# Statistics of the next input moved ahead, softplus in three steps, and a shorter tie rule, in a one-core kernel of AdaLN, Mamba and mixture of experts

## The chip, the cores and the metric

The kernel runs on one core of a Trainium2 chip. The time is the device time of one execution in microseconds (us). The kernel before has a median of 687.32 us over 3 runs (684.01 to 691.07). The execution that was profiled took 684.8 us, its span from the first to the last instruction being 683.1 us.

## What is computed

Eight sequences of 512 tokens with 128 features pass through two blocks. All values are fp32.

```python
mod = (silu(c) @ wmod)            # six rows per sequence: sa, ca, ga, sb, cb, gb
h = layernorm(x) * (1 + ca) + sa
# Mamba: d_inner 256, state 16, dt_rank 8
xz = h @ in_proj_w.T;  x, z = split(xz)
x = silu(conv1d(x) + conv_b)      # causal, 4 taps, per channel
dt, Bm, Cm = split(x @ x_proj_w.T)
delta = softplus(dt @ dt_w.T + dt_b)
h_t = h_(t-1) * exp(delta * A) + (delta * x) * Bm     # 256 x 16 states, 512 steps
y = sum_n(h_t * Cm) + x * D;  y = y * silu(z)
x = x0 + ga * (y @ out_proj_w.T)
# mixture: a shared expert and 8 experts, the two likeliest weighted by their softmax
h = layernorm(x) * (1 + cb) + sb
x = x + gb * (shared(h) + sum_e(weight_e * expert_e(h)))   # gelu(h @ w1 + b1) @ w2 + b2
```

When two experts have the same probability, the one with the lower index comes first.

## The kernel before

One sequence is called a batch (b). Its tokens are 4 tiles of 128 (NT); the 256 inner channels are 2 halves (Q). The recurrence of a batch is cut into 16 units (UN, `u` from 0 to 15): a unit is one half of the channels and two of the sixteen states, 128 partitions by 2 x 512 elements.

What a unit needs, engine by engine: ScalarE (ACT) computes the decay exp(delta * A) by two instructions of 128x511 (`decays`, L885); VectorE (DVE) multiplies into PSUM (`scan_input`, L1197) and runs the recurrence (`scan`, L1206); GpSimd (POOL) multiplies by C (`readout`, L433); TensorE (PE) adds the product, transposed, to y in PSUM by eight transposes (`y_add`, L516). There are 8 decay buffers and 4 state buffers, so that `scan(b, u)` waits for `y_add(b, u - 4)`. PSUM has one input buffer for the scan.

Every engine runs its own list of instructions in the order in which the functions `slots` issue them; there is no scheduler. `pipeline` calls `slots(b, a, n, m)` with four batches at different stages: b is scanned (all 16 units), a = b - 1 goes through the gate, the output projection and the mixture of experts, n = b + 1 through convolution, projections and softplus, m = b + 2 through its input statistics and normalisation. One such call is called a period here; after the first, b = 0 (no a), there are seven, five of them with all four, one without m (b = 6) and one without n and m (b = 7), and a tail for the last a.

The stages of a in a period, in order: `gate_y` (DVE), `g_transpose` (PE), `g_rows` (ACT), `out_proj` (PE), `att_rows` (ACT, L969), `att_transpose` (PE, L600), `residual` (DVE, L1226: the add, then mean and variance of x1), `make_rstd` (POOL, L420 and L423: the power -0.5), `x1hat` (DVE, L1244), `x1_transpose` (PE, L616), `h2_rows` (ACT, L992 and L995), `router` (PE, L624), `split_h2` and `logits` (DVE, L1310 and from L1254), 18 times `up` (PE, L645 to L647, three matmuls each) with `gelu` (ACT, L1014), `top2` (DVE, from L1268), then 8 times `down` (PE, L677), `mix_scaled` (ACT, L980) and `mix_add` (PE, L687). `gelu` and Exp need different tables of ScalarE. `keep_busy` (L611) is a row of transposes whose result nobody reads.

The stages of n: `conv_in`, `x_silu` (ACT, L906), `x_proj`, `dt_proj` (PE, L572, one for each half), `softplus_relu` and `softplus_abs` (ACT, L936 and L943), `softplus_exp` (ACT, L952), `softplus_log` (ACT, L957) and on DVE `make_delta` (L1170 to L1179). The softplus is relu(v) + e - ((1 + e) - 1) + ln(1 + e), with e = exp(-|v|). The stages of m: `load_x` (SP queue, L347), `stats` (DVE, from L1147), `make_rstd`, `xhat` (DVE, L1158).

In `readout` the flag `paced` makes POOL wait for the input of the next unit as well as for its own scan, so that the readout lies beside a scan and not beside a `scan_input`.

## Time and profile before

| | before |
|---|---|
| median of 3 runs | 687.32 us (684.01 to 691.07) |
| profiled execution | 684.8 us, span 683.1 us |
| busy: PE, DVE, ACT, POOL | 593.3, 598.3, 489.7, 320.2 us |
| chain that ended last, share of the span | PE 53%, DVE 31%, issue 7%, ACT 5%, POOL 2% |
| mean granted clock of TensorE | 0.955 of full speed |
| starts of `residual` (L1226), a = 0 to 7 | from 118.0 us to 636.6 us |

A busy time is the time in which an engine runs instructions. Two engines are busy for nearly nine tenths of the span, so neither alone tells what a shorter instruction is worth: for that one follows one period through all engines. In a timeline, a bracket behind an instruction gives the idle time of its engine ahead of it and the instruction whose end ended it. Consecutive instructions overlap by about a tenth of a microsecond, so that lengths can add up to a little more than the difference of the starts. The times of a timeline are counted from the start of the span.

### The profile page before, as it was taken

What the parts mean: (1) busy time and instruction counts of PE and PEld (TensorE: products, weight loads), DVE (VectorE), ACT (ScalarE), POOL (GpSimd) and SP (SyncE); (2) the same over time, 40 slices, a digit from 0 to 9 for tenths busy, and PEclk for the clock granted to TensorE, in tenths of its full rate; (3) what the DMA queues carried; (4) which work ended last, traced back from release to release, by engine and by line L of the source; (5) the groups of instructions that cost most, each with busy time, mean ns of one, the idle gap of its engine ahead of it and who ended that gap; (6) DMA issues with size and microseconds to landing.
All of it is one profiled execution on the core that took longest, in us unless ns stands there. A gap on an engine that the chain in (4) does not pass through costs nothing.

```text
span 683.1 us, 9767 instructions
## 1 busy us (share of the span) xinstructions
PE 593.3 (87%) x3646; PEld 466.5 (68%) x3646; DVE 598.3 (88%) x713; ACT 489.7 (72%) x861; POOL 320.2 (47%) x171
## 2 busy tenths in 40 slices
PE   5684478899989998999989998999979947998897
PEld 4243345689657965788567966787668936798686
DVE  5399999999999999999999999999998999798416
ACT  3689535999589976989589957998598925962460
POOL 1036556446654556446653656446543664464000
PEclk9787589999999999999999999999999968999999
DMA  7423333314432235133531343223522442220000
GB/s 221 161 92 140 123 139 142 125 70 169 163 128 82 108 128 184 62 124 124 173 124 63 124 160 138 83 103 124 179 103 70 176 156 83 103 78 16 1 1 16
DMA packets 26705, 77.87 MB, mean 114 GB/s; under 512 B 3025, under 2 KB 17570, under 8 KB 18466
## 3 DMA queue, kind: packets, MB, share of 16 engines
q1 hardware_dynamic: 26178, 76.82, 31.1%
q8 instruction: 29, 0.48, 0.3%
q10 hardware_dynamic: 480, 0.43, 0.2%
q14 instruction: 18, 0.15, 0.1%
HBM read 74.61 MB, written 2.62 MB: 113 GB/s over the span
## 4 chain that ended last, share of the span: by engine, by line
PE 53%; DVE 31%; issue 7%; ACT 5%; POOL 2%; DMA 1%; DVEq 0%; POOLq 0%; ACTq 0%
DVE state L1206 15%; PE psum L677 12%; PE psum L516 10%; DVE psum L1197 8%; PE psum L543 5%; PE psum L645 5%; PE psum L647 4%; PE psum L646 4%; PE psum L687 3%; POOL state L433 2%; PE psum L662 2%; PE psum L565 1%; ACT L866 1%; DVE out_sb L1244 1%; PE psum L799 1%
## 5 line engine op out<-in xcount | busy, mean ns | idle before, releaser
L433 POOL TENSOR_TENSOR state<-state,bc 128x1024 f32<-128x1024 f32 x127 | 300.1, 2363 | 291.8 <-DVE psum L1197 291.8
L1206 DVE TENSOR_TENSOR_SCAN state<-decay,psum 128x1024 f32<-128x1024 f32 x128 | 292.2, 2283 | 21.9 <-PE psum L516 9.5
L885 ACT ACTIVATE decay<-delta,a_neg 128x511 f32<-128x511 f32 x256 | 166.1, 729 | 10.4 <-DVE state L1206 10.3
L516 PE MATMUL psum<-ident,state 128*128 128x128 f32 x1024 | 139.0, 283 | 33.6 <-POOL state L433 33.4
L1197 DVE TENSOR_TENSOR psum<-bc,du 128x1024 f32<-128x1024 f32 x128 | 157.6, 1231 | 4.8 <-DVE state L1206 0.5
L516 PEld LDWEIGHTS psum<-ident,state 128*128 128x128 f32 x1024 | 120.3, 146 | 56.0 <-POOL state L433 44.9
L677 PE MATMUL psum<-down_w,h 128*128 128x128 f32 x896 | 109.9, 276 | 0.0
L677 PEld LDWEIGHTS psum<-down_w,h 128*128 128x128 f32 x896 | 104.4, 192 | 5.3 <-issue 5.3
L1014 ACT ACTIVATE h<-psum,vec 128x512 f32<-128x512 f32 x144 | 97.0, 688 | 2.1 <-PE psum L647 0.6
L980 ACT ACTIVATE gT_mix<-psum,w 128x128 f32<-128x128 f32 x224 | 64.8, 388 | 20.0 <-PE psum L687 14.4
L645 PE MATMUL psum<-h_hi,up_hi 128*128 128x512 f32 x144 | 59.2, 411 | 10.7 <-DVE h_lo L1310 6.7
L543 PE MATMUL psum<-h_sb,conv_in_wT 128*128 128x512 f32 x128 | 59.9, 614 | 8.8 <-ACT h_sb L895 8.8
L647 PE MATMUL psum<-h_hi,up_lo 128*128 128x512 f32 x144 | 57.7, 401 | 0.0
L646 PE MATMUL psum<-h_lo,up_hi 128*128 128x512 f32 x144 | 57.6, 400 | 0.0
L543 PEld LDWEIGHTS psum<-h_sb,conv_in_wT 128*128 128x128 f32 x128 | 24.3, 199 | 34.6 <-issue 25.4
L645 PEld LDWEIGHTS psum<-h_hi,up_hi 128*128 128x128 f32 x144 | 27.5, 191 | 20.5 <-DVE h_lo L1310 7.3
L687 PE MATMUL psum<-ident,gT_mix 128*128 128x128 f32 x224 | 33.9, 274 | 0.0
L647 PEld LDWEIGHTS psum<-h_hi,up_lo 128*128 128x128 f32 x144 | 27.4, 190 | 6.7
L646 PEld LDWEIGHTS psum<-h_lo,up_hi 128*128 128x128 f32 x144 | 27.6, 191 | 6.0
L687 PEld LDWEIGHTS psum<-ident,gT_mix 128*128 128x128 f32 x224 | 26.0, 141 | 1.5 <-ACT gT_mix L980 1.5
L611 PE MATMUL psum<-ident 128*128 128x128 f32 x210 | 26.2, 273 | 0.0
L906 ACT ACTIVATE du<-psum,vec 128x512 f32<-128x512 f32 x16 | 10.8, 687 | 21.2 <-PE psum L543 18.7
(151 smaller groups left out, 638.3 us busy)
## 6 DMA issues: line engine op xcount, KB each, us to landing
bc<-bc_rows SPq DMA_DIRECT2D x64, 1024.0 KB, 4.7
x_sb<-_attn_hidden_states_dram SPq DMA_DIRECT2D x9, 256.0 KB, 2.8
x<-_attn_hidden_states_dram SPq DMA_DIRECT2D x7, 256.0 KB, 3.0
out_dram<-out_sb SPq DMA_DIRECT2D x7, 256.0 KB, 2.4
h<-in_L_ffn_rw_dram SPq DMA_DIRECT2D x1, 1024.0 KB
bc_rows<-rows SPq DMA_DIRECT2D x8, 64.0 KB, 4.8
h<-in_L_wmod_dram ACTq DMA_DIRECT2D x1, 384.0 KB
h<-in_L_attn_in_proj_w_dram SPq DMA_DIRECT2D x1, 256.0 KB, 4.7
```

Of the source, the lines that this page charges most:

```text
L433: pool.tensor_tensor(state[:, u % STATE_RING, :, :], state[:, u % STATE_RING, :, :], bc[:, pair % BC_RING, 1, first:first + NU, :], ALU.mu ...
L516: last = nc.tensor.matmul(Y[q][:, t * P:(t + 1) * P], state[:, u % STATE_RING, s, t * P:(t + 1) * P], ident[:, :], start=False, stop=(u in ...
L543: last = nc.tensor.matmul(A[q], conv_in_wT[:, q, k, :], h_sb[:, k:k + L], start=(k == 0), stop=(k == KC - 1))
L645: nc.tensor.matmul(bank, high, h2_hi[:, :], start=True, stop=False)
L646: nc.tensor.matmul(bank, high, h2_lo[:, :], start=False, stop=False)
L647: nc.tensor.matmul(bank, low, h2_hi[:, :], start=False, stop=True).then_inc(up_done, 1)
L677: last = nc.tensor.matmul(A[j % 2][:, e * DM:(e + 1) * DM], h1[:, (group * EG + e) * HQ + q, ts], down_w[:, group * EG + e, q, :], start=( ...
L687: last = nc.tensor.matmul(OUTP[:, t * P:(t + 1) * P], mix[:, j % 2, e, :], ident[:, :], start=False, stop=(j == DOWNS - 1 and e == EG - 1) ...
L885: last = nc.scalar.activation(decay[:, r, s, 1:L], delta[:, b.p, q, 1:L], ACT.Exp, scale=a_neg[:, q, k:k + 1])
L1014: nc.scalar.activation(h1[:, m, :], UP_RING[m % 3], ACT.Gelu, bias=vec[:, bias:bias + 1]).then_inc(gelu_done, 1)
L1197: nc.vector.tensor_tensor(IN, bc[:, pair % BC_RING, 0, first:first + NU, :], du[:, b.p, q:q + 1, :].broadcast_to([P, NU, L]), ALU.mult).th ...
L1206: nc.vector.tensor_tensor_scan(state[:, u % STATE_RING, :, :].rearrange("p n t -> p (n t)"), decay[:, u % DECAY_RING, :, :].rearrange("p n ...
```

## The change

- `top2`: in place of a comparison for equality, one for greater, a product with the mask `before` and a sum, the probabilities are multiplied by `tie_scale` (1 - 2^-24 where the other index is lower, else 1) and compared once: two instructions of 128x256 in place of four.
- Softplus: ScalarE computes 1 + e (`softplus_one`) into the last two buffers of h1; DVE takes relu + e and then ((1 + e) - 1) less that sum after unit 4, and subtracts it from the logarithm after unit 7. The instruction L1173 goes. The first batch keeps the form of before. `gelu` of the last two h1 buffers waits until DVE has read them.
- DVE: `residual`, `stats` of m and `x1hat` come in one piece between units 2 and 3; `split_h2` and `logits` after unit 3 in place of unit 4. `stats` has a buffer of its own (`bn_in`).
- PE: `att_transpose` ahead of both `dt_proj`; `y_add` of unit 2 ahead of the first `keep_busy`; the two `keep_busy` have 8 and 10 transposes in place of 14 and 5 (12 in the last period).
- POOL: the readout of unit 2 isn't paced when there is an a, and both `make_rstd` follow it.
- ACT: the decays are computed 7 units ahead in place of 6, and two units rather than four of them stand between softplus and the gelus; the other two follow in the loop over the experts and at its end.

```diff
...
 GATE_MIN = 0.25
 STATE_RING = 4
 DECAY_RING = 8
-AHEAD = 6
+AHEAD = 7
...
-        before = sb("before", [P, E, E], mybir.dt.bfloat16)
+        tie_scale = sb("tie_scale", [P, E, E])
...
         bn = sb("bn", [P, NT, 6])
+        bn_in = sb("bn_in", [P, NT, 6])
...
+
+        one_plus_e = h1[:, M_UP - Q:M_UP, :]
...
+        sp_one = sem("softplus_one_plus_exp")
...
+        def delta_steps(n, k):
+
+            return k if n.i == 0 else 3 + 2 * (n.i - 1) + k
...
-            pool.memset(before[:, :, :], 1.0).then_inc(const_made, 1)
+            pool.memset(tie_scale[:, :, :], 1.0 - 2.0 ** -24).then_inc(const_made, 1)
...
+            pool.affine_select(out=tie_scale[:, :, :], in_=tie_scale[:, :, :],
+                               pattern=[[1, E], [-1, E]],
+                               compare_op=ALU.is_gt, fill=1.0, base=0,
...
                 for u in range(UN - 1):
                     if b:
-                        readout(b, u)
+                        readout(b, u, paced=not (a and u == 2))
                     if a and u == 2:
                         make_rstd(1, stats2_done, rstd2_eps, rstd2_done, a)
-                    if m and u == 5:
+                    if m and u == (2 if a else 5):
                         make_rstd(0, stats_done, rstd_eps, rstd_done, m)
...
+                if a:
+                    att_transpose(a)
                 if n:
                     dt_proj(n, 0)
-                if a:
-                    att_transpose(a)
-                if n:
                     dt_proj(n, 1)
                 if b and a:
                     y_add(b, 0)
                 if b:
                     y_add(b, 1)
-                if a:
-                    keep_busy(a, n, 14)
+                    y_add(b, 2)
+                if a:
+                    keep_busy(a, n, 8)
                     x1_transpose(a)
-                if b:
-                    y_add(b, 2)
-                if a:
-                    keep_busy(a, n, 5 if b else 12)
+                    keep_busy(a, n, 10)
                     router(a)
                     for k in range(M_UP):
...
+            def softplus_one(n):
+                if n.i >= 3:
+                    act.wait_ge(shared_done, n.i - 2)
+                act.wait_ge(sp_exp, n.i + 1)
+                nc.scalar.activation(one_plus_e, g_soft[:, :, :], ACT.Identity,
+                                     bias=1.0).then_inc(sp_one, 1)
+
...
-            def gelu(a, m):
+            def gelu(a, m, n=None):
                 act.wait_ge(up_done, M_UP * a.i + m + 1)
+                if n and m == M_UP - Q:
+                    act.wait_ge(delta_step, delta_steps(n, 2))
...
+                if n and n.i > 0:
+                    softplus_one(n)
+                if a:
+                    h2_rows(a)
+                if b:
                     decays(b, AHEAD + 1)
-                if a:
-                    h2_rows(a)
-                if b:
-                    decays(b, AHEAD + 2)
-                    decays(b, AHEAD + 3)
                 if a:
                     router_e(a)
                     load_gelu_table(a)
                     for k in range(M_UP):
-                        gelu(a, k)
+                        gelu(a, k, n)
                     weights_out(a)
...
                 for j in range(DOWNS - 1):
-                    if b and j < DOWNS - 2:
-                        decays(b, AHEAD + 4 + j)
+                    if b:
+                        decays(b, AHEAD + 2 + j)
...
-                    last = nc.vector.bn_stats(bn[:, t, :], x_sb[:, t, :])
+                    last = nc.vector.bn_stats(bn_in[:, t, :], x_sb[:, t, :])
...
                 for t in range(NT):
-                    last = nc.vector.bn_aggr(mean_var[:, 0, t, :], bn[:, t, :])
...
+            def relu_plus_exp(n):
                 d = delta[:, n.p, :, :]
                 dve.wait_ge(sp_relu, Q * n.i + Q)
                 dve.wait_ge(sp_exp, n.i + 1)
-                nc.vector.tensor_tensor(d, d, e, ALU.add).then_inc(delta_step, 1)
-                dve.wait_ge(delta_step, 3 * n.i + 1)
+                nc.vector.tensor_tensor(d, d, g_soft[:, :, :], ALU.add).then_inc(delta_step, 1)
+
+            def rounded_less_sum(n):
+                d = delta[:, n.p, :, :]
+                dve.wait_ge(delta_step, delta_steps(n, 1))
+                dve.wait_ge(sp_one, n.i)
+                nc.vector.scalar_tensor_tensor(out=d, in0=one_plus_e, scalar=1.0, in1=d,
+                                               op0=ALU.subtract, op1=ALU.subtract
+                                               ).then_inc(delta_step, 1)
+
+            def log_less(n):
+                dve.wait_ge(delta_step, delta_steps(n, 2))
                 dve.wait_ge(sp_ln, n.i + 1)
+                for q in range(Q):
+                    nc.vector.tensor_tensor(delta[:, n.p, q, :], skip[:, q, :],
+                                            delta[:, n.p, q, :], ALU.subtract
+                                            ).then_inc(delta_done, 1)
+
...
-                k = 8 * a.i
+                k = 6 * a.i
...
-                mine = pr[:, :, :].unsqueeze(3).broadcast_to([P, NT, E, E])
-                other = pr[:, :, :].unsqueeze(2).broadcast_to([P, NT, E, E])
-                nc.vector.tensor_tensor(gt_eq[:, 1, :, :, :], other, mine, ALU.is_equal
-                                        ).then_inc(prob_step, 1)
-                nc.vector.tensor_tensor(gt_eq[:, 0, :, :, :], other, mine, ALU.is_gt
-                                        ).then_inc(prob_step, 1)
+                nc.vector.tensor_tensor(
+                    gt_eq[:, 1, :, :, :], pr[:, :, :].unsqueeze(3).broadcast_to([P, NT, E, E]),
+                    tie_scale[:, :, :].unsqueeze(1).broadcast_to([P, NT, E, E]),
+                    ALU.mult).then_inc(prob_step, 1)
+                dve.wait_ge(prob_step, k + 4)
+                nc.vector.tensor_tensor(
+                    gt_eq[:, 0, :, :, :], pr[:, :, :].unsqueeze(2).broadcast_to([P, NT, E, E]),
+                    gt_eq[:, 1, :, :, :], ALU.is_gt).then_inc(prob_step, 1)
                 dve.wait_ge(prob_step, k + 5)
-                nc.vector.tensor_tensor(
-                    gt_eq[:, 1, :, :, :], gt_eq[:, 1, :, :, :],
-                    before[:, :, :].unsqueeze(1).broadcast_to([P, NT, E, E]),
-                    ALU.mult).then_inc(prob_step, 1)
-                dve.wait_ge(prob_step, k + 6)
-                nc.vector.tensor_tensor(gt_eq[:, 0, :, :, :], gt_eq[:, 0, :, :, :],
-                                        gt_eq[:, 1, :, :, :], ALU.add).then_inc(prob_step, 1)
-                dve.wait_ge(prob_step, k + 7)
                 nc.vector.tensor_reduce(rank[:, :, :], gt_eq[:, 0, :, :, :], AX.X,
                                         ALU.add).then_inc(prob_step, 1)
-                dve.wait_ge(prob_step, k + 8)
+                dve.wait_ge(prob_step, k + 6)
...
+                if a:
+                    residual(a)
+                if a and m:
+                    stats(m)
+                if a:
+                    x1hat(a)
                 if b:
                     scan_input(b, 3)
-                if a:
-                    residual(a)
                 if b:
                     scan(b, 3)
                 if a:
-                    x1hat(a)
+                    split_h2(a)
+                    logits(a)
                 if b:
                     scan_input(b, 4)
                     scan(b, 4)
-                if a:
-                    split_h2(a)
-                    logits(a)
+                if b and n:
+                    relu_plus_exp(n)
+                    rounded_less_sum(n)
...
+                if m and not a:
                     stats(m)
...
                 if n:
-                    make_delta(n)
+                    if n.i == 0:
+                        first_delta(n)
+                    else:
+                        log_less(n)
...
```

In the lists of instructions `h` stands for h1, h2 and h_sb, and a number behind x is how often a row follows itself. Two places show what moves. The first is DVE in a full period from the third scan (L1206, then L1241) on. Before:

```order
L1197 TENSOR_TENSOR psum<-bc,du 128x1024
L1226 TENSOR_TENSOR x<-psum,x 128x512
L1230 BN_STATS bn<-x 128x6 x4
L1233 MEMSET router_stats 128x1
L1235 BN_AGGR mean_var<-bn 128x2 x4
L1206 SCALAR_TENSOR_TENSOR state<-decay,psum 128x1024
L1244 TENSOR_SCALAR out_sb<-x,mean_var,rstd 128x128 x4
L1197 TENSOR_TENSOR psum<-bc,du 128x1024
L1206 SCALAR_TENSOR_TENSOR state<-decay,psum 128x1024
L1310 TENSOR_TENSOR h_lo<-h,h_hi 128x512
L1254 TENSOR_TENSOR gT_mix<-psum,router_bias 128x32
```

Now:

```order
L1261 TENSOR_TENSOR x<-psum,x 128x512
L1265 BN_STATS bn<-x 128x6 x4
L1268 MEMSET router_stats 128x1
L1270 BN_AGGR mean_var<-bn 128x2 x4
L1162 BN_STATS bn_in<-x_sb 128x6 x4
L1165 MEMSET router_stats 128x1
L1167 BN_AGGR mean_var<-bn_in 128x2 x4
L1279 TENSOR_SCALAR out_sb<-x,mean_var,rstd 128x128 x4
L1232 TENSOR_TENSOR psum<-bc,du 128x1024
L1241 SCALAR_TENSOR_TENSOR state<-decay,psum 128x1024
L1339 TENSOR_TENSOR h_lo<-h,h_hi 128x512
L1289 TENSOR_TENSOR gT_mix<-psum,router_bias 128x32
```

The input of unit 3 and its scan moved behind x1hat, the statistics of x_sb came in ahead of it, and one input and scan less stand ahead of h_lo.

The second is ACT in a full period, from the last instruction of softplus before the logarithm to the gelus, and then the end of the loop over the experts (L980, now L993). Before:

```order
L952 ACTIVATE g_soft<-skip 128x1024
L885 ACTIVATE decay<-delta,a_neg 128x511 x4
L992 ACTIVATE h<-psum,modT 128x512
L995 ACTIVATE h_hi<-psum,modT 128x512
L885 ACTIVATE decay<-delta,a_neg 128x511 x4
L1001 ACTIVATE gT_mix<-gT_mix 128x32
...
L895 ACTIVATE h_sb<-psum,modT 128x512
L980 ACTIVATE gT_mix<-psum,w 128x128 x4
L885 ACTIVATE decay<-delta,a_neg 128x511 x2
L980 ACTIVATE gT_mix<-psum,w 128x128 x4
```

Now:

```order
L958 ACTIVATE g_soft<-skip 128x1024
L891 ACTIVATE decay<-delta,a_neg 128x511 x2
L965 ACTIVATE h<-g_soft 128x1024
L1005 ACTIVATE h<-psum,modT 128x512
L1008 ACTIVATE h_hi<-psum,modT 128x512
L891 ACTIVATE decay<-delta,a_neg 128x511 x2
L1014 ACTIVATE gT_mix<-gT_mix 128x32
...
L891 ACTIVATE decay<-delta,a_neg 128x511 x2
L901 ACTIVATE h_sb<-psum,modT 128x512
L993 ACTIVATE gT_mix<-psum,w 128x128 x4
L891 ACTIVATE decay<-delta,a_neg 128x511 x2
L993 ACTIVATE gT_mix<-psum,w 128x128 x4
```

Ahead of the gelus two units of decays went and the instruction for 1 + e came; ahead of the last two pieces of the mixture one unit of decays was added.

## Rows read from the trace of the kernel before

**Rows 1.** The instructions of L1226 (seven of eight): lengths in ns, first and last start.

```profile
L1226 DVE TENSOR_TENSOR x<-psum,x x7: 684/685/692, 118.0 to 569.5; 128x512 f32<-128x512 f32 x7
```

**Rows 2.** One period: busy PE, PEld, DVE, ACT, POOL (instructions), clock, DMA share, GB/s.

```profile
343.20:418.20 75.00, 70.69 (x448) 55.67 (x447) 71.48 (x81) 61.65 (x111) 40.15 (x20) 1.00 0.34 122
```

**Rows 3.** Timeline of DVE, same period: start, length, engine, line, operation [idle before <-releaser].

```profile
343.25 0.69 DVE L1226 TENSOR_TENSOR x<-psum,x 128x512 f32<-128x512 f32 x1
...
345.18 2.25 DVE L1206 TENSOR_TENSOR_SCAN state<-decay,psum 128x1024 f32<-128x1024 f32 x1
347.35 1.09 DVE L1244 TENSOR_SCALAR out_sb<-x,mean_var,rstd 128x128 f32<-128x128 f32 x4
...
351.92 0.67 DVE L1310 TENSOR_TENSOR h_lo<-h,h_hi 128x512 fp32r<-128x512 f32 x1
...
357.24 0.42 DVE L1278 TENSOR_TENSOR gT_mix<-gT_mix 128x256 f32<-128x256 f32 x1
...
364.51 1.12 DVE L1158 TENSOR_SCALAR x_sb<-x_sb,mean_var,rstd 128x128 f32<-128x128 f32 x4 [0.40 <-POOL rstd L423]
...
367.29 2.29 DVE L1206 TENSOR_TENSOR_SCAN state<-decay,psum 128x1024 f32<-128x1024 f32 x1 [0.52 <-PE psum L516]
...
370.73 0.69 DVE L1173 TENSOR_SCALAR g_soft<-g_soft 128x1024 f32<-128x1024 f32 x1
```

**Rows 4.** Timeline of POOL, same period.

```profile
343.42 2.38 POOL L433 TENSOR_TENSOR state<-state,bc 128x1024 f32<-128x1024 f32 x1 [1.34 <-DVE psum L1197]
...
346.03 1.01 POOL L423 TENSOR_TENSOR rstd<-rstd,constants 128x4 f32<-128x4 f32 x1
```

**Rows 5.** Timeline of PE, same period.

```profile
340.56 1.12 PE L572 MATMUL psum<-rows,small_w 8*128 8x512 f32 x2
341.61 0.66 PE L600 MATMUL psum<-ident,h 128*128 128x128 f32 x4
...
348.49 0.66 PE L616 MATMUL psum<-ident,out_sb 128*128 128x128 f32 x4 [1.75 <-DVE out_sb L1244]
...
352.64 0.50 PE L645 MATMUL psum<-h_hi,up_hi 128*128 128x512 f32 x1 [0.89 <-DVE h_lo L1310]
```

**Rows 6.** Timeline of ACT, same period.

```profile
341.72 0.69 ACT L936 ACTIVATE delta<-psum,vec 128x512 f32<-128x512 f32 x1 [0.36 <-PE psum L572]
...
345.62 2.54 ACT L885 ACTIVATE decay<-delta,a_neg 128x511 f32<-128x511 f32 x4
349.19 0.78 ACT L992 ACTIVATE h<-psum,modT 128x512 f32<-128x512 f32 x1 [1.02 <-PE psum L616]
...
354.82 12.24 ACT L1014 ACTIVATE h<-psum,vec 128x512 f32<-128x512 f32 x18
...
379.24 1.14 ACT L980 ACTIVATE gT_mix<-psum,w 128x128 f32<-128x128 f32 x4 [0.79 <-PE psum L687]
...
394.29 1.14 ACT L980 ACTIVATE gT_mix<-psum,w 128x128 f32<-128x128 f32 x4 [0.57 <-PE psum L687]
```

**Rows 7.** Timeline of the SP queue, same period.

```profile
338.82 0.38 SPq L347 DMA_DIRECT2D x_sb<-_attn_hidden_states_dram  x1
```

**Rows 8.** The page, part 6: size and us from issue to landing.

```profile
x_sb<-_attn_hidden_states_dram SPq DMA_DIRECT2D x9, 256.0 KB, 2.8
```

**Rows 9.** Timeline of ACT, first period with a scan (40 to 108 us).

```profile
56.34 1.06 ACT L952 ACTIVATE g_soft<-skip 128x1024 f32<-128x1024 f32 x1
```

**Rows 10.** Timeline of DVE, the same first period.

```profile
54.25 2.29 DVE L1206 TENSOR_TENSOR_SCAN state<-decay,psum 128x1024 f32<-128x1024 f32 x1
```

**Rows 11.** Timeline of DVE, period of b = 6 (from 493.27 us).

```profile
517.52 2.29 DVE L1206 TENSOR_TENSOR_SCAN state<-decay,psum 128x1024 f32<-128x1024 f32 x1 [2.85 <-PE psum L516]
```

**Rows 12.** Timeline of DVE, last period, b = 7 (from 569.50 us).

```profile
594.70 2.29 DVE L1206 TENSOR_TENSOR_SCAN state<-decay,psum 128x1024 f32<-128x1024 f32 x1 [4.01 <-PE psum L516]
597.09 1.23 DVE L1197 TENSOR_TENSOR psum<-bc,du 128x1024 f32<-128x1024 f32 x1
```

**Rows 13.** One microsecond of the last period; columns as in Rows 2.

```profile
581.00:582.00 1.00, 1.00 (x4) 0.54 (x3) 1.00 (x1) 1.00 (x3) 1.00 (x1) 0.50 0.97 410
```

22 lines of the change are left out of this document (12 added, 10 removed).

## The prediction

> **What bounds the kernel now.** I begin with the busy times and the chain of waits, in the table ahead. They give no single bound: PE and DVE are both busy for nearly nine tenths, and the chain runs through both (53% and 31%). So I look for a repeating piece. The line of the residual add starts seven times from 118.0 to 569.5 [rows 1]; the first five distances are 75.0 us each, the last is 76.2, and one of them is the window of [rows 2]. In it PE is busy 70.7 of 75 us and DVE 71.5, with the PE clock at full speed; ACT has 61.7, POOL 40.2.
>
> The timelines show how the period closes. After the gate of batch a there is one path through all engines: projection, PE's transposes [rows 5], residual and x1hat on DVE [rows 3], the power on POOL [rows 4], ACT's two copies from 349.19 [rows 6], h_lo on DVE at 351.92, and the first up matmul at 352.64, for which PE had waited 0.89. From there PE runs nearly without a gap, first the ups with the gelus (354.82 on), then the eight pieces of the mixture, whose scaling on ACT goes from 379.24 to the last at 394.29 (several pieces are not shown) [rows 6]. This closed path is 75 us long. DVE's own list is nearly as long: its idle time in the period is mostly 0.40 for the power of m and 0.52 for PE ahead of scan 7 [rows 3]. Both must shrink for the period to shrink.
>
> **What DVE saves.** Per period: the add and subtract of 1 (0.69, with its gap 0.7), and two of four 128x256 instructions at 0.42 [rows 3], 0.8 together. The new three-operand instruction has no row of its size; I take it as long as the two-operand one over 1024 elements, 1.23 [rows 12]. It can't be under half of that by the fastest such row (0.69 for 1024 elements, one operand); the upper end, twice 1.23, would come from reading its two SBUF operands one after the other; it would use up DVE's slack below and add about 0.8 a period, +4.6 in all. The wait of 0.40 for the power of m goes, since stats moves six scans ahead. Its input must have landed: it is issued at 338.82 [rows 7] and needs 2.8 [rows 8], so it is there at 341.6, 2.5 before it is read. Two gaps of 0.13 between an input and its scan, so far filled by other work, come back.
>
> **The front, step by step** (times of the period shown). Scan 2 ends at 342.1, one scan input (1.23, overlapping by 0.1) before 343.25. The transposed rows come at 342.1 too: att_transpose was behind one dt_proj that began at 340.56, and now waits only for ACT's copy; PE's loss is about 0.8 idle. Residual now runs from 342.2; it takes 1.93 (343.25 to 345.18 [rows 3]) and ends at 344.1. The statistics of m are the same instructions without the add, 1.2, up to 345.35: they fit into the wait for the power. On POOL the unpaced readout starts at 342.1, not 343.42, takes 2.4 and ends at 344.5; the power follows as before, 1.25 behind (from 345.8 to 347.04 [rows 4]), so it is ready at 345.8. DVE idles 0.45, x1hat (1.09) ends at 346.9, and input and scan 3 (3.65) at 350.5.
>
> ACT meanwhile is later. Both dt_proj (1.05 each, start to start [rows 5]) now follow att_transpose, so relu, at 341.72 before, starts at 343.15. The chain relu to exp loses its idle 0.36 and reaches the decays at 346.55 in place of 345.62 [rows 6]. Now one unit of decays, half of 2.54, and the copy 1 + e, which I put at 1.0 from the exp over 128x1024 (1.06 [rows 9]; bounds one and two of ACT's 128x512, 0.7 and 1.4 [rows 6]), end at 348.85. x1_transpose, behind three products and eight fillers on PE, is done at 348.4. So ACT's copies start at 348.85 instead of 349.19: the front is bound by ACT, and the fast x1hat buys only 0.35.
>
> What does get earlier is h_lo: it was held by scan 4 until 351.92, and now needs only the copies, 350.4. PE's router ends at 351.4, and the ups start there, **1.25 earlier**; the logits wait 0.45 for the router and come 1.05 earlier, and with them the table load and the gelus.
>
> **The back.** PE, DVE's products and ACT shift by 1.05 up to 379.24. But two units of decays that stood ahead of the gelus now stand behind them. One comes in the loop ahead of the last pieces: 1.3 (half of 2.54, a little more where shapes alternate), of which the 0.57 idle at 394.29 [rows 6] hides a part. The last scaling starts at 394.29 - 1.05 + 1.3 - 0.57 = 393.97, or 0.1 sooner by the overlap of consecutive instructions, so the period shrinks by 0.3 to 0.45; I take **0.4**. The other unit follows the copy of the finished rows; it waits for scan 14 and delays the copies of the next convolution's first half, which have 2 us of slack because the second half is still on PE. DVE by itself ends softplus 0.8 to 0.9 earlier and waits the rest at the gate. Cover: the extra decays cost nothing more as long as PE is later than 393.9. The ring allows all of it: scan 9 needs its decay near 378, and ACT makes it behind the gelus at 372.
>
> **The sum.** Five full periods: -5 x 0.4 = -2.0. Period of b = 6: DVE stood 2.85 ahead of scan 7 for the product behind the ups [rows 11]. With the softplus work moved before it and the ups earlier the stall is gone; from there DVE was the bound until the next gate, and softplus ends at 522.1 in place of 524.1: -2.0. Period of b = 7: no softplus; residual waits for PE as before, h_lo now waits for scan 3, 0.7 earlier than behind scan 4; scan 7 (594.70, idle 4.01 [rows 12]) follows by -0.7. First period with a scan, b = 0, bound by DVE: the new position is too early there. Scan 4 ends at 56.54 [rows 10] but exp at 57.40 [rows 9], and 0.65 later now, since a seventh decay unit goes ahead of it; then ACT's decays and 1 + e before the second step. DVE waits 1.5 and 1.0 and saves 0.7: **+1.8**. The tail keeps its path: top2 there ends long before the weights are asked for, 0. Sum: -2.0 - 2.0 - 0.7 + 1.8 = **-2.9 us**. The profiled execution took 684.8, which gives 681.9; it lies 2.5 under the median, so the median goes from 687.3 to **684.4**.
>
> **Rivals.**
> - *POOL holds DVE up.* The power of m now runs on POOL from 345.9 to 347.1, beside x1hat; before, both powers ran beside scans [rows 3, 4]. If x1hat has to stand aside for one power (1.01), scan 3 and h_lo come 1.0 later; the ups and gelus are then 0.25 to 0.4 earlier only, the last scaling is 0.15 late, and five periods give +0.8 in place of -2.0 (b = 6 and 7 have no m): 684.4 + 2.8 = 687.2, no change. For it: no row shows an x1hat beside a POOL instruction. Against it: the readout beside the residual took 2.38 as others do [rows 4]. The Trainium skill, "SBUF — State Buffer", section "Who interferes with whom", says that a VectorE tensor_scalar in a two-port mode and a GpSimd instruction exclude each other for the whole instruction; by that rule this rival is right, and the unpaced readout, beside instructions with one SBUF operand, costs nothing. No row here shows whether x1hat is in such a mode.
> - *Nothing is given back.* If ACT's loop has more slack than I count, the period is DVE's, -0.9: 5 x 0.9 + 2.0 + 0.7 - 1.8 = -5.4, 681.9; with the front's two DVE waits also covered (-1.8 a period) -9.9, 677.4. Against it: the brackets on ACT show only 0.57 between the third and the last scaling.
> - *ACT becomes the bound.* If the copies at 349.19 come later, not 0.35 earlier (a longer 1 + e, or a wait of relu), every us there delays ups and gelus, and 1.3 - 0.57 = 0.7 is added behind them. The break-even is gelus 0.7 earlier than before. With gelus at their old time a period is 0.7 longer: 3.5 + 1.8 - 2.0 - 0.7 = +2.6, 689.9; with 1 + e and relu together 1 us worse, +7.6, 694.9. This is the one that ends slower.
> - *The PE clock falls.* In the last period it is at half speed at 581 us [rows 13] during the ups, after a stretch with long PE waits. The change puts 0.8 idle ahead of att_transpose and removes one filler. A dip in each period costs between 0.8 and 2.5 in the ups: +1 to +9, to 693. Against it: from 345 to 352 PE has less idle than before (1.75 ahead of x1_transpose goes to about nothing).
>
> **Numbers.** Forecast 0.42; POOL holds DVE 0.18; nothing given back 0.17; ACT bound 0.15; clock 0.08. The range goes from 678.5 (inside the second rival, and the spread of three runs) to 690.5 (ACT bound, first step). A measurement of this kernel can tell about 1%, 6.9 us, from no change: faster than 680.4 has 0.17, from the second rival and a low median; slower than 694.2 has 0.10; the rest 0.73.
>
> **What would show it.** Right: periods of 74.5 to 74.7 between residual adds; ups starting 9.2 behind the residual (352.64 - 343.25 = 9.4 before, with the residual itself 1.05 earlier); a new wait of DVE for POOL ahead of x1hat and for PE ahead of the logits; no wait ahead of the last scaling on ACT; in the first period two DVE waits for ACT after scan 4. Wrong: a period that shrinks by 0.9 or more (the loop had slack); x1hat or the power longer than 1.1 and 1.0 (POOL); ACT copying later than 7.0 behind the residual (ACT); a granted clock under full speed in the steady part. If the first period shows no wait for exp, the +1.8 was wrong.

## The result, and the profile after

The changed kernel takes **693.0 us** (median of 8 executions, 690.1 to 694.75) against 686.8 for the kernel before (8 executions, 684.01 to 691.07): ratio 1.0084, 95% interval 1.0053 to 1.0115. Run again later beside others of this study (c1_control below) it took 689.82, ratio 1.0049 [1.0017, 1.0080]. The two intervals overlap. So it is slower by 0.5 to 0.8%, where the forecast was 684.4 with a range up to 690.5; that the later 689.82 lies inside this range is no merit of the forecast, which had the sign wrong. The profiled execution took 694.75.

First the whole, by cores and clock, and one full period (b = 4) from gate to gate; the columns are those of [rows 2].

```profile
core 0: 692.8 us, clock 0.931
```

```profile
342.76:418.10 75.34, 71.72 (x447) 57.20 (x446) 70.33 (x77) 62.18 (x112) 40.09 (x21) 0.98 0.36 122
```

The clock over the whole execution was 0.955 before. A full period is 75.34, against the 75.0 of [rows 2]: DVE is busy 1.2 less, and still the period is longer. The clock in it is 0.98, in [rows 2] it was full.

The front of such a period on TensorE, which answers to [rows 5], and the same stretch by the microsecond:

```profile
346.44 1.98 PE L602 MATMUL psum<-g_soft,out_wT 128*128 128x512 f32 x4 [0.24 <-ACT g_soft L977]
349.21 0.66 PE L609 MATMUL psum<-ident,h 128*128 128x128 f32 x4 [0.78 <-ACT h L982]
349.79 1.98 PE L581 MATMUL psum<-rows,small_w 8*128 8x512 f32 x4
351.70 4.50 PE L525 MATMUL psum<-ident,state 128*128 128x128 f32 x24
...
356.92 0.60 PE L625 MATMUL psum<-ident,out_sb 128*128 128x128 f32 x4
...
359.06 1.06 PE L633 MATMUL psum<-router_sb,h 128*128 128x8 f32 x8 [0.45 <-ACT h_hi L1008]
359.97 0.48 PE L654 MATMUL psum<-h_hi,up_hi 128*128 128x512 f32 x1
```

```profile
351.00:352.00 1.00, 1.00 (x4) 0.30 (x3) 0.96 (x9) 1.00 (x2) 1.00 (x1) 0.88 0.00 0
352.00:353.00 1.00, 1.00 (x6) 1.00 (x5) 0.96 (x8) 1.00 (x3) 0.92 (x3) 0.50 0.00 0
353.00:354.00 1.00, 1.00 (x7) 1.00 (x6) 0.58 (x5) 0.97 (x2) 0.92 (x3) 0.50 0.00 0
354.00:355.00 1.00, 1.00 (x7) 1.00 (x6) 1.00 (x4) 1.00 (x3) 0.80 (x1) 0.50 0.00 0
```

PE has work without a gap from 349.21 to the router, and at about 351.8 its clock goes from full (2.4 GHz) to half (1.2 GHz) until 355.2. The 24 products of y_add take 4.50; with the clock full, in b1_wide_dt below, 2.84. x1_transpose stands behind them.

DVE and ACT in the same period, answering to [rows 3] and [rows 6]:

```profile
353.58 1.12 DVE L1279 TENSOR_SCALAR out_sb<-x,mean_var,rstd 128x128 f32<-128x128 f32 x4 [0.42 <-POOL rstd L432]
...
359.03 0.69 DVE L1339 TENSOR_TENSOR h_lo<-h,h_hi 128x512 fp32r<-128x512 f32 x1 [0.78 <-ACT h_hi L1008]
360.15 0.19 DVE L1289 TENSOR_TENSOR gT_mix<-psum,router_bias 128x32 f32<-128x32 f32 x1 [0.43 <-PE psum L633]
...
365.50 1.23 DVE L1188 SCALAR_TENSOR_TENSOR delta<-h,delta 128x1024 f32<-128x1024 f32 x1
```

```profile
350.95 0.69 ACT L942 ACTIVATE delta<-psum,vec 128x512 f32<-128x512 f32 x1 [1.80 <-PE psum L581]
...
357.55 0.78 ACT L1005 ACTIVATE h<-psum,modT 128x512 f32<-128x512 f32 x1 [0.92 <-PE psum L625]
...
362.47 12.20 ACT L1029 ACTIVATE h<-psum,vec 128x512 f32<-128x512 f32 x18
...
402.32 1.24 ACT L993 ACTIVATE gT_mix<-psum,w 128x128 f32<-128x128 f32 x4
```

ACT waits 0.92 for x1_transpose, h_lo waits 0.78 for ACT, and the first gelu comes at 362.47. The last scaling, at 402.32, has no idle ahead of it. POOL's second power ran beside x1hat (1.12; 1.09 in [rows 3]), and neither took noticeably longer:

```profile
352.53 1.01 POOL L432 TENSOR_TENSOR rstd<-rstd,constants 128x4 f32<-128x4 f32 x1
...
353.79 1.01 POOL L432 TENSOR_TENSOR rstd<-rstd,constants 128x4 f32<-128x4 f32 x1
```

The second full period (b = 2) is the longest, 79.0. DVE stands there for a load, and the SP queue shows why; this answers to [rows 7]:

```profile
202.97 0.87 DVE L1162 BATCH_NORM_STATS2 bn_in<-x_sb 128x6 f32<-128x128 f32 x4 [5.38 <-DMA x_sb<-_attn_hidden_states_dram]
```

```profile
186.97 0.43 SPq L393 DMA_DIRECT2D gate_row<-gateT  x1
195.75 0.32 SPq L395 DMA_DIRECT2D gate_row_sb<-gate_row  x1
196.11 2.60 SPq L369 DMA_DIRECT2D bc_rows<-rows  x1
200.37 0.38 SPq L355 DMA_DIRECT2D x_sb<-_attn_hidden_states_dram  x1
```

SP waits there until the gate row's store has landed, 8.8 us, before it issues the next two transfers, and the load of x stands behind them. From the page, part 6 (size, us from issue to landing):

```profile
gate_row<-gateT SPq DMA_DIRECT2D x1, 0.5 KB, 8.8
```

Last the first period, answering to [rows 9] and [rows 10]:

```profile
58.06 1.23 DVE L1182 TENSOR_TENSOR delta<-delta,g_soft 128x1024 f32<-128x1024 f32 x1 [1.60 <-ACT g_soft L958]
...
60.23 1.23 DVE L1188 SCALAR_TENSOR_TENSOR delta<-h,delta 128x1024 f32<-128x1024 f32 x1 [0.94 <-ACT h L965]
```

From gate to gate (the start of gate_y, one per batch; the column b = k runs from the gate in that period to the next) the profiled executions compare as follows, in us; "rest" is from the last gate to the end.

```
                 first gate  b=1    b=2    b=3    b=4    b=5    b=6    b=7    rest   span
before            109.71    75.03  75.03  75.19  75.01  75.02  75.90  68.74  53.47  683.1
after             111.26    77.11  79.03  75.36  75.34  75.32  76.35  68.09  54.94  692.8
c1_control        110.67    75.06  79.61  75.37  75.34  75.36  74.69  67.36  54.94  688.4
e0_gate_late_only 110.76    77.11  75.40  75.34  75.34  75.35  74.68  67.31  54.91  686.2
e2_gate_late_dt   110.88    74.22  74.24  73.45  74.20  74.55  73.34  67.44  54.88  677.2
```

Two words are used below for the parts of a period: the front is the stretch from the gate to the first gelu, the back the one from there to the next gate.

c1_control is the same program as after: b = 1 and b = 6 differ by 2.05 and 1.66 between the two, the first gate, b = 2 and b = 7 by 0.6 to 0.7, b = 3 to 5 and the rest by nothing. In b = 1 and b = 6 of after the half clock lasts twice as long, and y_add takes 5.38. So b = 1 and b = 6 of the first profile are partly chance (e0_gate_late_only has the 77.11 of b = 1 again), and the second is the better account: +1.0 up to the first gate, +4.6 in b = 2, +0.2 to +0.3 in each of b = 3 to 5, -1.2 in b = 6, -1.4 in b = 7, +1.5 in the rest; together +5.3. The profile of before, from which this is counted, is one of its best executions: its clock of 0.955 is the highest of 31, the lowest being 0.933.

### The profile page after: what moved, and what is told of

It reads as the page before. It is cut to its first block, busy times and chain, and to the rows that moved or that the text cites. A ratio compares the mean times of both kernels' runs of the same rounds, so it can differ in the third digit from the quotient of the medians.

```text
span 692.8 us, 9748 instructions
## 1 busy us (share of the span) xinstructions
PE 608.0 (88%) x3639; PEld 481.4 (69%) x3639; DVE 589.0 (85%) x690; ACT 493.8 (71%) x868; POOL 320.0 (46%) x171
## 4 chain that ended last, share of the span: by engine, by line
PE 42%; DVE 28%; ACT 17%; issue 6%; DMA 3%; POOL 2%; DVEq 0%; POOLq 0%; ACTq 0%; SPq 0%
DVE state L1241 12%; DVE psum L1232 9%; PE psum L525 8%; ACT decay L891 5%; PE psum L552 5%; ACT gT_mix L993 4%; PE psum L686 3%; PE psum L654 3%; PE psum L655 3%; PE psum L656 3%; PE psum L602 2%; PE psum L581 2%; PE psum L564 2%; POOL state L442 2%; PE psum L574 2%
## 5 line engine op out<-in xcount | busy, mean ns | idle before, releaser
L1241 DVE TENSOR_TENSOR_SCAN state<-decay,psum 128x1024 f32<-128x1024 f32 x128 | 292.5, 2285 | 14.8
L525 PE MATMUL psum<-ident,state 128*128 128x128 f32 x1024 | 151.1, 302 | 30.6 <-POOL state L442 30.6
L525 PEld LDWEIGHTS psum<-ident,state 128*128 128x128 f32 x1024 | 132.6, 157 | 54.2 <-POOL state L442 41.4
L993 ACT ACTIVATE gT_mix<-psum,w 128x128 f32<-128x128 f32 x224 | 65.5, 402 | 15.3 <-PE psum L696 9.7
L620 PEld LDWEIGHTS psum<-ident 128*128 128x128 f32 x203 | 24.8, 149 | 0.5 <-issue 0.5
```

Source lines behind the costliest of these rows:

```text
L525: last = nc.tensor.matmul(Y[q][:, t * P:(t + 1) * P], state[:, u % STATE_RING, s, t * P:(t + 1) * P], ident[:, :], start=False, stop=(u in ...
L993: last = nc.scalar.activation(mix[:, j % 2, e, :], A[j % 2][:, e * DM:(e + 1) * DM], ACT.Copy, scale=w9[:, t, group * EG + e:group * EG + ...
L1241: nc.vector.tensor_tensor_scan(state[:, u % STATE_RING, :, :].rearrange("p n t -> p (n t)"), decay[:, u % DECAY_RING, :, :].rearrange("p n ...
```

## The experiments

Each was compared with executions of the kernel before on the same chip (medians 685.2 to 687.1 there), so the ratios compare better than the medians.

```
kernel               median  ratio to before [95%]       clock of the profiled one
a1_dt_first          688.72  1.0022 [0.9996, 1.0049]     0.935
a2_fill              689.08  1.0035 [1.0004, 1.0065]     0.938
a3_before_att        688.69  1.0037 [1.0003, 1.0071]     0.933
a4_gate_row          687.15  1.0014 [0.9979, 1.0048]     0.937
b1_wide_dt           688.94  1.0032 [1.0003, 1.0062]     0.940
b2_y2_late           688.46  1.0022 [0.9993, 1.0052]     0.933
b3_decay_gap         688.02  1.0006 [0.9980, 1.0032]     0.938
b4_four              681.85  0.9909 [0.9872, 0.9946]     0.945
c1_control           689.82  1.0049 [1.0017, 1.0080]     0.935
c2_gate_first        686.03  1.0002 [0.9975, 1.0029]     0.938
c3_before_top2       686.23  1.0013 [0.9992, 1.0034]     0.950
c4_three             680.67  0.9932 [0.9907, 0.9956]     0.942
d1_pad_each          688.88  1.0026 [0.9992, 1.0060]     0.945
d2_pad_once          690.41  1.0062 [1.0032, 1.0093]     0.947
d3_three_y2          681.43  0.9935 [0.9902, 0.9968]     0.939
d4_three_dt          680.24  0.9909 [0.9875, 0.9944]     0.945
e0_gate_late_only    686.59  1.0000 [0.9968, 1.0031]     0.935
e2_gate_late_dt      677.28  0.9864 [0.9827, 0.9901]     0.944
```

### The wait for x in b = 2

**a4_gate_row** leaves only the store of the gate row there:

```diff
                 if b and b.i == 1:
                     sp.wait_ge(gate_steps, 4)
                     sp.dma_start(gate_dram, ...).then_inc(gate_stored, 16)
+                if b and b.i == 2:
                     sp.wait_ge(gate_stored, 16)
```

> The changed kernel with the wait for the one-time round trip of the gate row (store, wait, load of the broadcast row) taken out of the second full period: the store stays, the wait and the load follow one period later, where the store has long landed. In the changed kernel the load of the input of batch 3 is issued at 200.37 behind it, and VectorE waits 5.38 us for that load. If that queue is the cause, this wait shrinks to under 0.5, the second full period goes from 79.0 to about 75.4, and the time from 693.0 to about 689.4. If the load is late by itself (the memory, or the store of rows ahead of it), the wait moves and the time stays at 692 to 693.

```profile
193.50 0.38 SPq L355 DMA_DIRECT2D x_sb<-_attn_hidden_states_dram  x1
```

```profile
196.72 0.87 DVE L1163 BATCH_NORM_STATS2 bn_in<-x_sb 128x6 f32<-128x128 f32 x4 [2.16 <-DMA x_sb<-_attn_hidden_states_dram]
```

```profile
194.83 5.38 PE L526 MATMUL psum<-ident,state 128*128 128x128 f32 x24
...
201.12 0.60 PE L626 MATMUL psum<-ident,out_sb 128*128 128x128 f32 x4
```

The period fell to 77.10, not 75.4. DVE still waited 2.16 for x: the load was issued at 193.50, 8.6 behind the store of the projected rows. But this wait is not what held the period. The half clock lasted twice as long there, y_add took 5.38, and x1_transpose came 15.79 behind the gate without idle ahead of it, as in b = 1 of after (15.78), which took 77.11 with no load to wait for. The same late load costs time where PE isn't late: in b4_four below DVE waits 2.31, and b = 2 takes 75.33 where b = 4 takes 73.79. **e0_gate_late_only** moves the whole block: `b.i == 1` becomes `b.i == B - 2`.

> The changed kernel with the gate row's whole block (store, wait, load) two periods from the end, where no x is loaded any more, and nothing else. Theory 1 (the store of 512 separate values holds up what is queued behind it, first of all the store of the projected rows and with it the load of x): no wait for x is left in the second full period, it becomes as long as the others, 75.1 to 75.4 in place of 79.0 and 79.6, and against the changed kernel's ratio of 1.005 to 1.008 the ratio to before falls to 0.998 to 1.002, 685 to 687. Theory 2 (the load comes late there by itself): a wait of 2 or more stays, the ratio stays at 1.002 to 1.005.

```profile
187.46 0.32 SPq L369 DMA_DIRECT2D bc_rows<-rows  x1
191.94 0.38 SPq L355 DMA_DIRECT2D x_sb<-_attn_hidden_states_dram  x1
```

```profile
196.81 0.28 DVE L1270 BATCH_NORM_AGGREGATE mean_var<-bn 128x2 f32<-128x6 f32 x3
197.01 0.84 DVE L1162 BATCH_NORM_STATS2 bn_in<-x_sb 128x6 f32<-128x128 f32 x4
...
198.68 1.12 DVE L1279 TENSOR_SCALAR out_sb<-x,mean_var,rstd 128x128 f32<-128x128 f32 x4 [0.41 <-POOL rstd L432]
```

Theory 1, in every point: the load comes 4.5 behind the store of the rows, bn_stats follows without a wait, b = 2 takes 75.40, and the ratio is 1.0000. Between c1_control and this kernel lie 4.2 us in b = 2, between after and this kernel 3.6. The ratio of the changed kernel was 1.0084 and 1.0049; the interval of e0_gate_late_only, 0.9968 to 1.0031, lies apart from the first and overlaps the second, so the profile is the stronger witness. **The second full period's load is the largest part of the loss.** The store of the gate row is what holds the queue. It writes 128 single values (the expectation's "512" are its bytes): these 0.5 KB took 8.8 us from issue to landing, 9.0 where they are moved to. In a4_gate_row, whose list doesn't wait for that store in this period, the load still came 8.6 behind the store of the rows instead of 4.5 (3.3 to 6.6 in b = 3 of before, after, c1_control and a4_gate_row).

### The first period

**c2_gate_first** (a4_gate_row, and in the period without a batch a the two softplus steps behind unit 7):

```diff
-                if b and n:
+                if b and n and a:
                     relu_plus_exp(n)
                     rounded_less_sum(n)
 ...
                     else:
+                        if not a:
+                            relu_plus_exp(n)
+                            rounded_less_sum(n)
                         log_less(n)
```

> The changed kernel with the gate row's wait out of the second full period and the first period's softplus work behind unit 7. Theory 1 (VectorE's waits of 1.60 and 0.94 lengthen the first period one to one): 2.0 to 2.5 under the gate row alone (687.15), so about 684.9, and the first gate comes some 58.7 behind the first copy of the projected rows, in place of 61.1. Theory 2 (the waits only move to another engine): 686.5 to 687.5.

In its profile the first gate comes 58.71 behind ACT's first copy of projected rows in that period (49.70 to 108.41), in after 61.07 (50.19 to 111.26), before 60.08. That copy doesn't come at the same place in DVE's list before and after; counted from DVE's scan 4, the last one ahead of the moved work, it is 54.72 here, 57.09 in after and in c1_control, and 55.46 before. Both waits are gone, and 2.4 us with them. The times don't show it: the ratio went from 1.0014 to 1.0002 (0.8 us, the medians by 1.1), well inside the intervals; in the rest of that profile b = 4 took 76.97 with the half clock twice as long.

### Is it DVE's list that sets the period?

**c3_before_top2** is the kernel before with the new tie rule alone (that part of the change's diff).

> The kernel before with the shorter tie rule of the change and nothing else: two 128x256 instructions less on VectorE in each period, 0.9 us. Theory 1 (the loop through the front and ScalarE's scalings sets the period, VectorE's own list doesn't): VectorE waits that much longer for TensorE at scan 7 or at the gate, full periods stay at 75.0, the time at 686 to 687, ratio 0.998 to 1.001. Theory 2 (VectorE's list sets the period): full periods 74.1 to 74.5, the time some 5 lower, 681 to 683.

```profile
369.00 2.29 DVE L1207 TENSOR_TENSOR_SCAN state<-decay,psum 128x1024 f32<-128x1024 f32 x1 [1.27 <-PE psum L517]
```

Theory 1. DVE waits 1.27 for PE ahead of scan 7, where the kernel before waited 0.52 [rows 3]; full periods are 74.96 to 75.00. In one period (b = 4) DVE is busy 70.70 in place of 71.49: of the 0.79 saved, 0.75 went into this wait.

### The clock and the front

Three kernels change what TensorE does ahead of the fall. **a1_dt_first** puts the first dt_proj ahead of att_transpose again, **a2_fill** puts fillers into the pause:

```diff
+                        pe.wait_ge(zs_done, 2 * n.i + 2)
+                        for k in range(7):
+                            nc.tensor.transpose(A[1][:, 0:P], ident[:, :], ident[:, :])
                     att_transpose(a)
```

**b1_wide_dt** gives dt_proj 40 rows: `dt_wT[2 * NS:2 * NS + R, q, :]` becomes `dt_wT[0:2 * NS + R, q, :]`, likewise its other operand.

> The changed kernel with one thing put back: TensorE gives the first dt_proj ahead of att_transpose again. In the changed kernel the granted clock is 0.50 for some 3 us of every full period, behind a pause of 0.78 us ahead of att_transpose. Theory 1 (the pause that the new order opened lets the clock fall): with dt_proj in the pause the clock stays 1.00 there, the 24 products of y_add take about 2.8 us instead of 4.50, full periods come down from 75.35 to about 75.0, and the time from 693.0 to about 690.5. Theory 2 (it is the two thin dt_proj and three y_add in one run, whatever stands ahead of them): the dips stay, 692 to 693.5. Theory 3 (the dips cost nothing, ACT's added decays set the longer period): the dips go or stay, and the periods remain at 75.3.

> The changed kernel with seven more filler transposes of the identity between out_proj and att_transpose, where TensorE stands idle for 0.78 us in a full period. Theory 1 (pause): the clock stays 1.00 through dt_proj and y_add, ups start some 0.7 earlier, 690.5 or a little less, as good as dt_proj ahead. Theory 2 (thin products): dips as before, about 693. Theory 3 (ACT's decays): the clock heals and full periods stay at 75.3, about 692.5.

> The changed kernel with dt_proj over 40 rows of its operands in place of 8 (the 32 rows more have zero weights, so the sum is the same). The runs so far showed half a clock behind the two dt_proj with fillers in the pause ahead of them and with the first of them ahead of att_transpose, so the pause alone is not the cause. Theory 1 (two products that use 8 of 128 rows, close together, let the clock fall): with five times the rows the granted clock of full periods stays 1.00 or falls in fewer of them, the whole execution's clock rises from 0.933 to 0.95 or more, and the time falls from 693.0 to 689 to 691. Theory 2 (the rows of the operands don't count; the stretch is at the brink, and where in it the clock is looked at decides): no difference, clock 0.931 to 0.937, 692 to 694.

```profile
351.00:352.00 1.00, 1.00 (x3) 0.51 (x4) 0.86 (x2) 0.00 (x0) 0.94 (x2) 1.00 0.06 16
352.00:353.00 1.00, 1.00 (x5) 0.24 (x3) 0.96 (x9) 0.92 (x2) 1.00 (x1) 1.00 0.00 0
353.00:354.00 1.00, 1.00 (x8) 1.00 (x7) 0.96 (x8) 1.00 (x3) 0.92 (x3) 0.64 0.00 0
354.00:355.00 1.00, 1.00 (x6) 1.00 (x6) 0.58 (x6) 0.97 (x2) 0.92 (x3) 0.50 0.00 0
```

```profile
350.43 2.84 PE L525 MATMUL psum<-ident,state 128*128 128x128 f32 x24
```

```profile
358.00:359.00 1.00, 1.00 (x6) 0.82 (x5) 0.93 (x4) 0.47 (x2) 0.00 (x0) 0.97 0.32 131
359.00:360.00 1.00, 1.00 (x4) 0.82 (x3) 0.87 (x2) 1.00 (x1) 0.30 (x1) 0.50 0.00 0
```

In a2_fill PE is busy without a gap from 347.57 on, at full clock, and the half clock comes all the same. In a1_dt_first it comes in b = 1, 2, 4, 5 and 6 of its profile, not in b = 3 (73.95), and the periods with it in y_add take 74.7: 0.65 better than in the changed kernel, though not by the clock; the whole front comes that much earlier (ups 16.55 behind the gate, 17.20 there). In b1_wide_dt the half clock comes at 359, in the ups, instead of in y_add; y_add takes 2.84 and the period 74.9 to 75.0 (b = 3 to 5). So all three theories of these expectations fall in part: the clock falls without the pause and it falls without the thin products (in b4_four below, with 40 rows, it falls in y_add again, in b = 5 and 6), and yet the half clock does cost time, by where it falls. The two were taken away one at a time, never both at once. b1_wide_dt and, below, c4_three against b4_four (8 rows against 40: ratios 0.9932 and 0.9909, intervals overlapping) show no worth of the wider rows that can be measured.

The other side is the kernel before with its TensorE untouched but for one thing. **a3_before_att** moves att_transpose ahead of both dt_proj, as the change does. **d1_pad_each** and **d2_pad_once** add one DVE instruction in each full period, or one in all:

```diff
+                if a and b and n:
+                    nc.vector.memset(pad[:, :], 0.0)
                 if a:
                     split_h2(a)
```
```diff
+                if a and a.i == 0:
+                    nc.vector.tensor_reduce(pad[:, 0:1], up_hi[:, 0:7, :].bitcast(F32), AX.XY,
+                                            ALU.add)
                 if b:
                     scan_input(b, 0)
```

> The kernel before with one thing of the change alone: att_transpose ahead of both dt_proj. Theory 1: TensorE now waits about 0.8 for ScalarE's copy in each full period and the granted clock falls to 0.50 behind it, as in the changed kernel; the time rises from 686.8 by 1 to 3 us, to 688 to 690. Theory 2: less than that, since no y_add(2) was moved up: 686.5 to 688 without dips. Theory 3: no change of time, 686.8, dips or not, since TensorE had 1.75 idle ahead of x1_transpose.

> The kernel before with one more instruction on VectorE in each full period, a memset over 128x256 of an unused tile ahead of h_lo, and nothing else: TensorE's order and its operands stay, each period only gets some 0.3 us longer. Theory 1 (moment: the clock falls where a moment at which it is judged meets the stretch of out_proj, dt_proj and transposes, and periods of 75.0 keep missing it): half clock appears in several full periods, the execution's clock goes from 0.955 to 0.935 to 0.945, the time rises by more than the 6 x 0.3 of the padding, to 688 to 692. Theory 2 (order and kind of TensorE's work): no half clock in full periods, clock 0.95 to 0.955, the time 687.5 to 688.5 by the padding alone. If the memset is shorter than 0.15, neither is tested.

> The kernel before with one instruction more in all, a reduction over 128x1792 on VectorE at the start of the first full period (its result is not used): the whole rest comes once some 1.9 us later, with periods as long as before. Theory 1 (moment): half clock in full periods in some or all executions, clock under 0.95, time 689 to 692. Theory 2 (order): clock 0.95 to 0.955 with none in full periods, time 686.2 + 1.9 = about 688.

a3_before_att has the half clock in every full period, at 344 in b = 4; PE is busy from 341.23 on, but stood idle ahead of that, as in the changed kernel:

```profile
341.23 0.66 PE L600 MATMUL psum<-ident,h 128*128 128x128 f32 x4 [0.78 <-ACT h L968]
```

The periods are 75.2 to 75.4 instead of 75.0 to 75.2. d1_pad_each (the memset takes 0.27) has periods of 75.24 to 75.41 in b = 1 to 4 without a half clock, and then it twice in b = 5 (76.05) and once in b = 6 (76.68; 75.90 before). d2_pad_once (the reduction takes 2.00) has one in b = 1 and 2 and none in the fronts and ups of 3 to 6:

```profile
130.00:131.00 1.00, 1.00 (x4) 0.76 (x3) 0.87 (x2) 1.00 (x1) 0.12 (x1) 0.50 0.93 385
131.00:132.00 1.00, 1.00 (x4) 0.81 (x3) 1.00 (x1) 0.99 (x4) 1.00 (x1) 0.50 1.04 410
132.00:133.00 1.00, 1.00 (x3) 0.74 (x3) 1.00 (x1) 0.70 (x2) 1.00 (x1) 0.50 0.39 148
```

b = 1 and 2 take 75.78 and 75.77 there, b = 3 to 5 75.01 and 75.02: **a half clock in the ups costs 0.76**. TensorE's work and its order were those of before. So a shift in time alone can bring half clocks (theory 1 of both), if not in every period. The executions of the kernel before are not all alike either: their clock goes from 0.933 to 0.955 in 31 of them, so that one profile can't tell a shift from chance; the ten executions of d2_pad_once, at a ratio of 1.0062 and clocks of 0.945 to 0.952, speak for the shift. The Trainium skill ("TensorE: Matmul & The Clock Gate", Part 1) says that how many matmuls of the same kernel run at the low clock differs from run to run, with the moment of its start; the clocks here differ from run to run too. What remains open is why the changed kernel's order meets the half clock in every period. Neither the pause nor the thin products alone account for it; a3_before_att shows that att_transpose ahead of both dt_proj is enough to bring it into every full period of the kernel before, a1_dt_first that putting the first dt_proj back is not enough to take it away.

**What the half clock costs in the changed kernel** can be read from one profile. In c1_control the stretch from gate to first gelu is 18.79 in b = 1, where the half clock came later, in the ups, and 19.71 in b = 3 to 5, where it is in y_add. Before it was 19.85. From first gelu to next gate it is 55.65, before 55.17, and 56.27 with a half clock in the ups. So a half clock costs 0.9 in y_add and 0.6 in the ups.

A full period without any can be seen in c2_gate_first, whose code in b = 3 is the changed kernel's (first gelu at 18.67):

```profile
260.72:335.05 74.33, 70.06 (x447) 55.54 (x446) 70.23 (x77) 62.09 (x112) 39.31 (x21) 1.00 0.34 121
```

It takes 74.33, 0.7 less than the 75.0 of [rows 2]. **Free of the half clock, the change does shorten a full period.**

**b2_y2_late** takes work from the stretch ahead of x1_transpose:

```diff
                     y_add(b, 1)
-                    y_add(b, 2)
                 if a:
-                    keep_busy(a, n, 8)
+                    keep_busy(a, n, 2)
                     x1_transpose(a)
-                    keep_busy(a, n, 10)
+                if b:
+                    y_add(b, 2)
+                if a:
+                    keep_busy(a, n, 3 if b else 11)
```

> The changed kernel with y_add(2) behind x1_transpose again, 2 fillers ahead of x1_transpose in place of 8, and 3 behind y_add(2) in place of 10. Theory 1 (the half clock costs time because 24 products of y_add and the fillers stand ahead of x1_transpose in it): x1_transpose comes at about 355.3 in place of 356.92 of the period from 342.76, ScalarE's copy no longer waits 0.92 for it, ups start about 0.9 earlier, a full period falls from 75.35 to 74.5 or 74.9, and the time from 693.0 to 688 to 691, with the dips still there. Theory 2 (ScalarE, with a unit of decays more behind the gelus, sets the period): periods stay at 75.3 and the time at 692.5 to 693.

Full periods b = 3 to 5 took 74.32, 74.78 and 74.92, as theory 1 had it. In b = 3 the half clock falls in y_add, and the first gelu still comes at 18.67, in place of 19.71 in c1_control: with a third of y_add behind x1_transpose and six fillers fewer ahead of it, the half clock there costs nothing. The median 688.46 lies at the lower end of theory 1's times, 1.4 under c1_control, with b = 2 at 80.8.

### ACT's decays

**b3_decay_gap** makes one unit of decays while ACT waits for dt_proj, so that one less is left for the loop of scalings:

```diff
+                if b and a:
+                    decays(b, AHEAD)
                 for q in range(Q):
                     ... relu, abs, exp
-                    decays(b, AHEAD)
+                    decays(b, AHEAD + 1)      # before softplus_one
 ...
-                    decays(b, AHEAD + 1)
+                    decays(b, AHEAD + 2)      # behind h2_rows
 ...
-                        decays(b, AHEAD + 2 + j)
+                        decays(b, AHEAD + 3 + j)      # j < DOWNS - 2
```

> The changed kernel with one unit of decays brought forward into the 1.80 us that ScalarE waits for dt_proj, so that of the two units that the change put behind the gelus one stands ahead of them again. Theory 1 (the extra unit in the loop with the mixture's scaling costs 0.5 us a full period, since the last scaling comes without idle and TensorE waits 0.50 for it): the stretch from the first gelu to the next gate shrinks from 55.6 to 55.1, the full period from 75.35 to 74.9, the time from 693.0 to about 690.5. Theory 2 (the half clock ahead of x1_transpose sets the period, ScalarE has room): less than 0.2 a period, 692 to 693.

```profile
347.46 1.32 ACT L891 ACTIVATE decay<-delta,a_neg 128x511 f32<-128x511 f32 x2
349.36 0.69 ACT L942 ACTIVATE delta<-psum,vec 128x512 f32<-128x512 f32 x1 [0.58 <-PE psum L581]
```

```profile
399.30 1.14 ACT L993 ACTIVATE gT_mix<-psum,w 128x128 f32<-128x128 f32 x4 [0.59 <-PE psum L696]
```

The unit fits: relu still waits 0.58 behind it. The last scaling has its idle of 0.59 again, and the stretch from first gelu to gate is 55.12 where no half clock is in it, 0.5 less than in the control: theory 1 for the back. Full periods are 74.19, 73.80 and 74.80. The 73.80 is the one without a half clock.

### Together

**b4_four** has the gate row's edit of a4_gate_row, the first period, the decays and dt_proj over 40 rows; **c4_three** the same over 8 rows; **d3_three_y2** is c4_three with y_add(2) late, **d4_three_dt** is c4_three with dt_proj ahead of att_transpose, and **e2_gate_late_dt** is that with the whole gate block late.

> The changed kernel with four edits together: the gate row's wait out of the second full period, the first period's softplus work behind unit 7 where its operands are ready (VectorE waits 1.60 and 0.94 there), dt_proj over 40 rows, and the unit of decays in ScalarE's gap. If the parts add up: 687.15 with the gate row alone, less 2.0 for the first period, less 2.5 for the decays, and up to 2 less for the clock if the rows count: 681 to 683. If the first period's waits only move to TensorE or ScalarE, and the rows don't count, 684.5 to 686.

> The changed kernel with the gate row, the first period and the decays as in the fastest so far (681.85), but dt_proj over 8 rows as before. Theory 1 (40 rows keep the clock up in some periods): granted clock 0.937 to 0.94 in place of 0.945, a dip in more of the full periods, 682.5 to 684.5. Theory 2 (rows don't count): 681.5 to 682.3 with the same clock.

> The fastest version so far (gate row, first period, decays; 680.67) with y_add(2) behind x1_transpose and two fillers ahead of it. Theory 1 (where the half clock meets y_add, it delays x1_transpose and so the ups; with a third less work there it doesn't): full periods that were 74.8 come to 74.3, time 678.5 to 680. Theory 2 (ScalarE's 1 + e and VectorE's scan 3 hold h_lo at the same place): periods as before, 680 to 681.5.

> The fastest version so far with the first dt_proj ahead of att_transpose again. In the changed kernel this alone shortened full periods from 75.35 to 74.7. Theory 1 (TensorE's front is still on the path): relu and y_add come earlier by 0.4 to 0.7, full periods fall to 73.8 to 74.3, time 678 to 679.5. Theory 2 (the later residual, 0.35, takes back what dt_proj gives, since VectorE's scan 3 now holds h_lo): 680.5 to 682.

> The fastest version (first period, decays, dt_proj ahead) with the gate row's whole block two periods from the end. Theory 1: the second full period falls from 76.2 to 73.8 to 74.3, the time from 680.2 by some 2 to 678 to 679, ratio 0.986 to 0.990. Theory 2: nothing moves, ratio 0.990 to 0.993.

b4_four came as added up. c4_three fell under both of its theories' figures, and no wider rows are needed. d3_three_y2 gave nothing that the times can show. Its profile has theory 1's full periods (b = 3 to 5: 74.36, 73.80, 73.81, in c4_three 74.84, 74.84, 74.34), the first gelu at 18.67 to 18.68 even where the half clock falls in y_add, and now bound by ACT; but in b = 2 DVE waited 4.42 for x, c4_three 3.84, and that period took 78.99 against 76.86. The gate row's edit of a4_gate_row doesn't cure the late load. d4_three_dt: 680.24 against 680.67, full periods 74.2, 74.2 and 74.7 instead of 74.8, 74.8 and 74.3, but the difference in the median is within its scatter; theory 1 holds in two of the three periods, neither in the time. **e2_gate_late_dt is the fastest: 677.28, ratio 0.9864 [0.9827, 0.9901]**, 9 us under the kernel before, and b = 2 takes 74.24. This line shows what a full period is with full clock throughout (the first of two, b = 3 and b = 4):

```profile
259.34:332.79 73.45, 70.53 (x447) 55.52 (x446) 70.13 (x77) 62.25 (x112) 39.52 (x20) 1.00 0.35 124
332.79:406.99 74.20, 71.84 (x447) 56.73 (x446) 70.14 (x78) 62.30 (x112) 40.86 (x21) 0.98 0.36 127
```

> The changed kernel itself once more, unchanged. Each single edit to it so far gave 687.2 to 689.1, 4 to 6 us under its 693.0, though the traces name only 2 to 4 for each. Theory 1 (the 693.0 stands, and each edit also moves the work against the moments at which the clock falls): 692 to 694, ratio to before 1.007 to 1.011. Theory 2 (the 693.0 was in part the state of that chip or hour): 689.5 to 691.5, ratio 1.003 to 1.006; then each edit's gain is to be counted from this figure.

c1_control decided how the gains are to be counted. Against 693.0 every edit had seemed worth 4 to 6 us; against its 689.82 (theory 2) dt_proj ahead, fillers and wide rows are worth about 1 us, y_add(2) late 1.4, and the gate row, moved by one period or to the end, and the decays 2 to 3. The interval of each of these single edits overlaps that of c1_control, so no single one is certain by its time; those of the combined kernels, b4_four to e2_gate_late_dt, lie clear of it.

## Why the prediction was wrong

**The step that failed in size is "Its input must have landed".** The prediction read one period, where the load is issued at 338.82, and took it for all. In b = 2 the queue is behind the gate row's store. Before, stats read x some 17 us later in the period, and the late load cost nothing; the change moved the reader ahead of it. Worth: b = 2 grew by 4.0 and 4.6 where -0.4 was forecast, and taking the store away gave back 3.6 and 4.2. The timeline of SP before shows that load at 198.81, 14 behind the gate at 184.74 instead of 4 to 7, so it could have been read:

```profile
183.78 0.43 SPq L385 DMA_DIRECT2D gate_row<-gateT  x1
...
198.81 0.38 SPq L347 DMA_DIRECT2D x_sb<-_attn_hidden_states_dram  x1
```

**The other is the clock.** The rival "The PE clock falls" had the effect and a chance of 0.08; its argument against (less idle ahead of the ups than before) rested on idle as the cause, and a2_fill shows the fall without idle ahead of it. So the forecast took the half clock at nothing in the full periods, and b = 3 to 5 came 0.2 to 0.3 longer instead of 0.4 shorter. Its price was right in order of size: 0.9 with the half clock in y_add, 0.6 to 0.8 with it in the ups. Its sum was not: five dips of 0.8 to 2.5 on top of 684.4 give 688.4 to 696.9, where "to 693" stands; even the least of it is a slower kernel, and the range ended at 690.5.

**The front was right.** Gelus 1.05 earlier were forecast; without a half clock ahead of them they come at 18.67 to 18.79 in place of 19.85. With one it is 0.14. DVE's wait for the power was forecast as 0.45 and is 0.42, its wait for the router 0.45 and is 0.42 to 0.43 with the half clock in y_add (0.39 without, in c1_control's b = 1).

**The back was nearly right.** Two terms, 1.3 - 0.57, gave +0.7 less the overlap; the stretch grew by 0.48. Without the half clock a full period would be 18.79 + 55.65 = 74.44, or -0.6, where -0.4 was forecast; the one that was seen, in c2_gate_first, is 74.33. The changed kernel itself had a half clock in every full period of both its profiles.

**The first period was right**: +1.8 forecast; from scan 4 to the first gate it is +1.63 in both profiles, with waits of 1.60 and 0.94 where 1.5 and 1.0 stood in the working. (The gate itself is +1.55 and +0.96 late, since scan 4 comes 0.1 and 0.7 earlier than before.) b = 7 was right too (-0.7 forecast, -0.65 and -1.38). b = 6 (-2.0) had the sign in one profile, -1.21, and not in the other, +0.45; there too it is the half clock, for in a2_fill, where the stretch up to the gelus and the ups has none, b = 6 takes 73.72, 2.2 less than before.

**The rivals.** *POOL holds DVE up* is refuted: x1hat took 1.12 and the power 1.01 side by side. By the rule quoted there from the Trainium skill the two would have excluded each other if x1hat were in a two-port mode; no run here shows whether it is. *Nothing is given back* in its first form (the period is DVE's) is refuted by c3_before_top2. *ACT becomes the bound* is half true: ACT is what costs 0.5 in the back, but the front was held by PE at half clock, since ACT waited for x1_transpose; at full clock it is bound by ACT, as forecast (its copies at 13.78 without idle).

**The rest**, +1.5 behind the last gate, was not in the sum. In the profile of before the ups of the last batch run at full clock and in all others compared above at half clock. Kernels without any of the moved work have it too: a3_before_att, d1_pad_each and d2_pad_once 54.95 to 55.02, c3_before_top2 56.1 with a half clock twice as long. So it belongs to the clock and not to the change. Two readings of the working were off and changed nothing: the first five distances between residual adds are not all 75.0 (the third is 75.2), and the statistics of m moved three scans ahead, not six.

## What to carry to other kernels

When work is moved ahead, look up when its input lands in every period and not in one: a single slow transfer, queued once, is enough to use up the gain of all of them. A saving on a busy engine is worth nothing until the closed path through the others is shortened with it, and there the waits of each engine (here ACT's 1.8 for dt_proj) are the places for work that has to go somewhere. Where the clock changes with the moment, one profile is no measure of a period; run the same kernel twice before an edit's gain is counted. And work that must end before a hand-over to another engine is best kept short where the clock may fall: moving a third of y_add behind x1_transpose, with six fillers fewer, took away the 1.0 that a half clock cost there.

## What the runs showed of the hardware that was not expected

- The granted clock fell to half with PE busy in every microsecond ahead of it (a2_fill, from 347.57 to the fall at 353.3), and with one 2.00 us instruction more on another engine there were falls that the profile of before had not (d2_pad_once).
- A store of 128 single values (0.5 KB) took 8.8 us in after, 9.0 in e0_gate_late_only and 9.6 before, and held up the transfers queued behind it; 64 KB of projected rows take 3.9 at the median.
- An ACT activation that adds 1 to 128x1024 takes 1.04, and DVE's new instruction, with three operands of which two are tensors in SBUF, 1.23, as long as its two-operand product over the same (L1182).
